# The first six steps of an attention loop in another order: value products first, the last query product behind them, two evacuations a step later

## What is computed

```
h = maximum(layernorm(x), 0)
q, k, v = h @ Wq.T + bq, h @ Wk.T + bk, h @ Wv.T + bv        # 8 heads of 32
scores  = (q @ k.T) * 32**-0.5 * (adj + adj)                  # per head, 1024 x 1024
x = x + softmax(scores) @ v @ Wo.T + bo
```

## Time and profile before

| | |
|---|---|
| median of three runs | 2977.01 us (2976.28 to 2977.42) |
| the profiled execution | 2976.45 us |
| its span, first to last instruction | 2974.6 us |
| TensorE busy | 2929.9 us (98%) |
| VectorE busy | 1869.7 us (63%) |
| ScalarE busy | 1476.8 us (50%) |
| GpSimd busy | 719.9 us (24%) |
| scores, L1292 | 1024 matmuls, 372.8 us |
| transposes, L1314 | 4096 matmuls, 539.0 us |
| masked maximum, L794 | 512, 622.5 us, 1217 ns each |
| exponential, L1050 | 512, 590.2 us, 1153 ns each |

### The profile page before, as it was taken

The page is one execution under the profiler, slowest core; times in us unless marked ns, Lnnn a source line. Parts: engine busy times, 40 slices in busy tenths (PEclk is TensorE's granted clock), DMA queues, the critical chain, the costliest instruction groups (busy, mean ns, idle before and its releaser), DMA issues.

```text
span 2974.6 us, 63498 instructions
## 1 busy us (share of the span) xinstructions
PE 2929.9 (98%) x23040; PEld 2376.7 (80%) x23040; DVE 1869.7 (63%) x4154; ACT 1476.8 (50%) x2761; POOL 719.9 (24%) x1305
## 2 busy tenths in 40 slices
PE   8999999999999999999999999999999999999999
PEld 6787787887878878788788886888868888688886
DVE  3797427974278742887428874388643886438862
ACT  1783317833178332883328732387323873238722
POOL 0343003420034201342013420134201341014410
PEclk9999999999999999999999999999999999999999
DMA  5202212022120231201311113111222021220200
GB/s 175 93 2 93 81 69 93 2 93 100 54 90 7 88 119 42 83 31 64 135 39 70 57 48 125 58 51 63 61 107 78 32 77 69 84 78 30 83 8 15
DMA packets 95317, 204.29 MB, mean 69 GB/s; under 512 B 10512, under 2 KB 41616, under 8 KB 94992
## 3 DMA queue, kind: packets, MB, share of 16 engines
q1 hardware_dynamic: 93456, 195.76, 18.0%
q0 software_dynamic: 1536, 4.20, 0.4%
HBM read 136.75 MB, written 8.65 MB: 49 GB/s over the span
## 4 chain that ended last, share of the span: by engine, by line
PE 82%; DVE 12%; ACT 3%; issue 2%; DMA 0%; DVEq 0%; ACTq 0%; SPq 0%
PE ps L1126 39%; PE ps L1314 15%; PE ps L1343 8%; PE ps L1292 8%; PE ps L1407 7%; PE ps L1482 4%; DVE junk L836 3%; DVE stats L633 1%; DVE h L852 1%; DVE dn L845 1%; DVE h L870 1%; PE ps L1166 1%; DVE shiftB L867 1%; ACT Uh L1093 1%; DVE Ul L678 1%
## 5 line engine op out<-in xcount | busy, mean ns | idle before, releaser
L794 DVE CUSTOM_DVE_ANT_0 Z<-ps,adjN 128x1024 f32<-128x1024 f32 x512 | 622.5, 1217 | 44.5 <-PE ps L1292 36.9
L1050 ACT ACTIVATE Z<-Z,nm 128x1024 f32<-128x1024 f32 x512 | 590.2, 1153 | 5.2 <-POOL nm L570 5.2
L1314 PE MATMUL ps<-ident,Z 128*128 128x128 f32 x4096 | 539.0, 275 | 2.2 <-ACT Z L1050 1.2
L1314 PEld LDWEIGHTS ps<-ident,Z 128*128 128x128 f32 x4096 | 463.7, 140 | 91.2 <-issue 42.5
L1292 PE MATMUL ps<-kS,qS 128*128 128x512 f32 x1024 | 372.8, 446 | 2.3 <-issue 1.8
L582 POOL TENSOR_SCALAR H<-adjN 128x128 fp32r<-128x128 f32 (+1 forms) x456 | 317.5, 696 | 0.0
L570 POOL TENSOR_TENSOR nm<-nm,minus 128x1 f32<-128x1 f32 x512 | 97.1, 190 | 557.0 <-DVE nm L794 556.6
L1126 PE MATMUL ps<-mh,adjT 128*128 128x256 f32 x1024 | 223.6, 379 | 0.8 <-issue 0.8
L1126 PE MATMUL ps<-v,P 128*128 128x257 f32 x1024 | 223.6, 379 | 0.0
L1126 PE MATMUL ps<-hT,t3T 128*128 128x512 f32 x512 | 221.0, 592 | 0.0
L1126 PEld LDWEIGHTS ps<-v,P 128*128 128x128 f32 x1024 | 193.9, 189 | 31.8 <-issue 3.8
(11 more groups left out here) (183 smaller groups left out, 5894.9 us busy)
## 6 DMA issues: line engine op xcount, KB each, us to landing
adjT<-adjT_in SPq DMA_DIRECT2D x8, 4096.0 KB, 13.2
adjN<-adj_in SPq DMA_DIRECT2D x8, 4096.0 KB, 17.2
adjT<-adjT_in SPq DMA_DIRECT2D x8, 2048.0 KB, 11.8
qS<-qhi SPq DMA_DIRECT2D x112, 128.0 KB, 2.1
qS<-qlo SPq DMA_DIRECT2D x112, 128.0 KB, 2.1
adjT<-adjT_in SPq DMA_DIRECT2D x8, 1536.0 KB, 6.4
xn<-x_in SPq DMA_DIRECT2D x8, 1024.0 KB, 5.8
out<-x SPq DMA_DIRECT2D x8, 1024.0 KB, 4.9
```

Of the source, the lines that this page charges most:

```text
L794: dve.tensor_tensor_reduce(Z[:, u % ZS], ps[:, 2 * (u % 2):2 * (u % 2) + 2].rearrange("p a n -> p (a n)"), adjN[:, u // HEADS], SCORE_SCAL ...
L1050: act.activation(Z[:, u % ZS], Z[:, u % ZS], ACT.Exp, bias=nm[:, u:u + 1], accum_out=sm[:, u:u + 1]).then_inc(exps.sem, 1)
L1314: mm = pe.transpose(ps[:, turn_bank((u, s)), rows(a)], Z[:, u % ZS, rows(NT // 2 * s + a)], ident[:])
```

## The change

Tables for each engine take the place of `BESIDE`. On TensorE, value products 1, 2 and 3 stand in steps 0, 2 and 3, and the last query product in step 4, where it waits for all four copies of values (it uses their bank). On ScalarE the copies of value products 1, 2 and 3 stand in steps 1, 2 and 3, each ahead of the step's evacuation. The upper part of the last query product is taken in step 5, ahead of the evacuations, and on VectorE the lower part in step 6, ahead of the evacuation of unit 3. ScalarE's evacuations of units 2 and 3 (`LATE`) are made one step later: step 3 has none, step 4 has unit 2, step 5 has units 3 and 4. The wait of value product 2 for the lower part is gone; the first weighted values wait for it instead of for the copies.

```diff
--- before.py
+++ after.py
@@ -315,10 +315,17 @@
         PARTS = (NT,)
 
 
-        BESIDE = {1: ("v", 1), 2: ("q", KQ_FIRST + 1), 4: ("v", 2), 5: ("v", 3)}
+        VALUES_AT = {0: 1, 2: 2, 3: 3}
+        COPY_VALUES_AT = {1: 1, 2: 2, 3: 3}
+        QUERY_AT, UPPER_AT, LOWER_AT = 4, 5, 6
+        LATE = (2, 3)
 
         BACK = (range(0, PTA), range(PTA, PTA + ZS), range(PTA + ZS, NT))
         STEPS = UNITS + HEADS + 3
+
+        def copied_by_act(u):
+
+            return [n for n in (u - 2, u - 1) if 0 <= n < UNITS and n + (2 if n in LATE else 1) == u]
 
         def turned(u):
 
@@ -796,8 +803,8 @@
                                                  nm[:, u:u + 1]).then_inc(zs.sem, 1)
                     if u == 1:
                         lower_kq(KQ_FIRST)
-                    if u - 2 in BESIDE and BESIDE[u - 2][0] == "q":
-                        lower_kq(BESIDE[u - 2][1])
+                    if u == LOWER_AT:
+                        lower_kq(KQ_FIRST + 1)
                     if (t := tile_due(u, NORMALISE)) is not None:
                         normalise(t)
                     if (t := tile_due(u, ADD)) is not None:
@@ -1049,15 +1056,15 @@
                         act.wait_ge(*nms(b, u + 1))
                         act.activation(Z[:, u % ZS], Z[:, u % ZS], ACT.Exp, bias=nm[:, u:u + 1],
                                        accum_out=sm[:, u:u + 1]).then_inc(exps.sem, 1)
-                    if u - 1 in BESIDE and BESIDE[u - 1][0] == "q":
-                        upper_kq(BESIDE[u - 1][1])
-                    if 1 <= u < UNITS + 1:
-                        evacuate(u - 1)
+                    if u == UPPER_AT:
+                        upper_kq(KQ_FIRST + 1)
+                    if u in COPY_VALUES_AT:
+                        copy_v(COPY_VALUES_AT[u])
+                    for n in copied_by_act(u):
+                        evacuate(n)
                     if u == 0:
                         upper_kq(KQ_FIRST)
                         copy_v(0)
-                    if u in BESIDE and BESIDE[u][0] == "v":
-                        copy_v(BESIDE[u][1])
 
                 act.activation(hh[:, :, D:HW], ones[:, 0:2 * NT].rearrange("p (t c) -> p t c", c=2), ACT.Copy).then_inc(ones_h.sem, 1)
                 for t in range(NT):
@@ -1220,8 +1227,6 @@
                         pe.wait_ge(*lasts(b, 4))
                     else:
                         pe.wait_ge(*vs(b, n))
-                    if n == 2:
-                        pe.wait_ge(*lo_s(b, len(KQ)))
                     for i in range(2):
                         mm = product(ps[:, 7, i * D:(i + 1) * D], [(hT1[:, c, rows(2 * n + i)], Wv1[:, c]) for c in range(DT)])
                     mm.then_inc(v_ps.sem, 1)
@@ -1330,7 +1335,7 @@
                         pe.wait_ge(*PT_act(b, by_act(HPG * g + HPG - 1)))
                         t = g // GROUPS
                         if g == 0:
-                            pe.wait_ge(*vs(b, NT // 2))
+                            pe.wait_ge(*lo_s(b, len(KQ)))
                         if g % GROUPS and t < NT - 1:
                             pe.wait_ge(*Rss(b, t + 1))
                         if g % GROUPS == 0 and t:
@@ -1385,13 +1390,11 @@
                     for part in range(len(PARTS)):
                         if (g := group_due(u, WEIGH + part)) is not None:
                             weighted_values(g, part)
-                    if u in BESIDE:
-                        what, n = BESIDE[u]
-                        if what == "v":
-                            project_v(n)
-                        else:
-                            pe.wait_ge(*vs(b, 2))
-                            project_kq(n)
+                    if u in VALUES_AT:
+                        project_v(VALUES_AT[u])
+                    if u == QUERY_AT:
+                        pe.wait_ge(*vs(b, NT // 2))
+                        project_kq(KQ_FIRST + 1)
                     if u > 0 and (n := turned(u)) is not None:
                         transposes(n)
                     if (t := tile_due(u, SPREAD)) is not None:
```

## The result

The changed kernel takes **2957.41 us** (median of four runs, 2953.71 to 2958.21) beside 2976.66 us of the kernel before. The ratio is 0.9936 with a 95% interval of 0.9924 to 0.9948: 19 us faster. Forecast were 2956.0 us and 2951 to 2964. The profiled execution took 2953.71 us, the lowest of the four.

The account below looks back on a forecast made before the run. TensorE, 82% of the chain, idles in each sample's first stretch. Winning 2.24 us there and 0.38 in the first tile, 2.62 per sample, 21.0 over eight, gives a median of 2956.0 us, range 2951 to 2964.

Parts of the forecast that it names:

- The first stretch: From the scores pair of unit 2 to first weighted values, per sample: 16.87 us instead of 19.11, 2.24 us won.
- the walk: Start-to-start schedule of the first sample on TensorE, ScalarE and VectorE, from measured distances: weighted values 0 at 110.74, not 112.98.
- S10: TensorE's scores pair of unit 10: at 110.10, waiting for VectorE's masked maximum of unit 8, 0.25 us behind TensorE's own list.
- The new waits: Last query product's wait for all copies: nothing, 0.47 us margin; weighted values' wait for lower half: met 3.9 us early.
- The late evacuations: ScalarE's evacuations of units 2 and 3, a step later: free, hidden by transposes and scores; otherwise 0.2 to 0.5 us each.
- the bound of 2950 us: Fastest case: waits and VectorE's chain cost nothing, TensorE's own list takes 16.14 us, 0.73 less per sample, 6 in all.
- The second term: First tile behind the first weighted values: VectorE's debt from inverting sums after exponential 7 shrinks, 0.38 us per sample won.
- rival B: Chain right, but the first tile's debt stays or value product to scores costs more: 1.9 to 2.2 us, 2961; chance 0.21.
- C: VectorE's turn 6 becomes the bound, upper half later than 105.11: if 1.25 us late, gain 11 us, 2966; chance 0.10.
- D: TensorE's clock falls in the stretch of transposes and scores behind the last query product: slower, 2986; chance 0.04.
- E: Plain loop is really held by VectorE and takes the lead back, leaving 0.5 us or less, 2973; chance 0.05.

## Why the prediction was right

**The first stretch.** Forecast 16.87 us, measured 17.11; the mis-sized term is one step of the walk. A scores pair to a product I took as 0.44 us, from two pairs and a product that took 0.99 together. Measured are 0.54 (91.39 to 91.93) and 0.55 (97.13 to 97.68), so value products 1, 2 and 3 came 0.10, 0.17 and 0.22 us later than in the walk (3.19 for 3.02 us behind S2 at the second, 6.29 for 6.07 at the third). It would have been more, but a product to the next transposes took 1.75 us (94.58 to 96.33) where I took 1.82. The copy of values 3 so stood at 8.22 us behind S2 instead of the walk's 8.00. The row I read held a product behind two pairs; the distance of one pair to what follows stood beside it in the prediction, as 0.55 to the next scores or transposes. From that copy on the walk held to the hundredth: 8.23 us from the copy of values 3 to S10 forecast (101.87 to 110.10) and measured (99.61 to 107.84), through exponential 4, evacuation 2, exponential 5, the upper half, the lower half, Z7 and Z8.

**The new waits.** The wait for all four copies ahead of the last query product cost nothing, as taken: no idle time is marked there. The weighted values' wait for the lower half cost nothing either (lower half at 103.56, weighted values at 108.50). The late evacuations were free, and the kernel without them shows that the one of unit 3 is more than free: I had priced them as a cost hidden by other work, not as what keeps the upper half early. That step was weak though not wrong: the prediction prices what they could cost, 0.2 to 0.5 us each, and not what they save. Without them 1.88 of the 2.03 us are lost.

**S10.** The prediction says that S10 comes 0.25 us later than TensorE's own list would allow. Its own steps say more: T5 at 107.49 and 0.79, 0.55 and 0.79 give 109.62, and S10 stands at 110.10, which is 0.48. Measured are 0.57 us, over three places: 0.17 at S9, 0.14 at T6 and 0.26 at S10 (0.96, 0.69 and 1.05 where plain are 0.79, 0.55 and 0.79), and taking the lower half out of the way gave back 0.54. The 0.26 at S10 alone is near the stated 0.25 by chance. The sum of TensorE's own list was wrong in the same place: the steps give 16.34 us and not 16.14, and 17.11 less 0.57 gives 16.54 as measured, so the bound of 2950 us lay too low. The forecast does not hang on either, as it went by the chain to S10.

**The second term.** Forecast 0.38 us, measured 0.38 by the sums (3.01 us over 8) and 0.40 in S13 to S14. Exponential 7 came 1.48 us ahead of the weighted values, forecast 1.36. Half of rival B, that the debt stays, fell here; its other half, a dearer step, is what happened in a small way, at S to product instead of V to S. The two together give 2.41 us per sample for 2.62, 19.3 for 21.0 us.

**The other rivals.** C had the right mechanism and not the size: the chain behind the upper half has no slack, and the kernel without late evacuations shows the price, 1.88 us lost for 1.88 us of lateness. D, the clock, did not occur: 1.00 in the 5.38 us of transposes and scores from 102.46 to 107.84. The rule in the Trainium skill, "TensorE: Matmul & The Clock Gate", section "Part 4: PE-mode transpose", that the full clock does not engage for transposes, is not borne out for this mixture. But a scores pair stands behind every eight transposes, in this stretch and in the row of 114.86 that the prediction held against the rule. What transposes alone would do no run shows. E, that the plain loop takes the lead back, fell: nothing of the lead was lost between weighted values 1 and the next sample (339.1 us on the mean for 339.3). The transfers of the second half of the queries caused no mark either.

## What to carry to other kernels

Taking a stop out of the list of the engine that ends the stretch pays only as far as no other engine's list puts it back: here the new order of products alone won 0.16 us of the first stretch, and with one evacuation made late 2.0 us. Write that engine's list down with one measured start-to-start distance per pair of operations, and then the lists of the engines that feed it, since the next bound is a sum on one of those. Look at what stands behind an instruction that must wait: moving one evacuation of 0.6 us behind the exponential and the upper half that were queued behind its wait was worth 1.9 us per sample. An edit of a loop's rhythm must be priced in its last round too, where the work beside it is of another size; keep it to the round that gains.

## What was not expected

**S2 is late in some samples**, by 0.1 to 1.2 us, and by nothing in others (0.79 us behind T0 is the plain distance). Which ones changes from run to run: three to six of eight, 2.1 to 4.6 us in all. The profile marks a transfer of key operands (kS) at some of them and "issue" at others, but the landing times say the same of all. The chain of waits of the changed kernel's first sample has

```profile
86.52 4.62 DMA kS<-klo
```

S2 starts at 91.39, 0.25 us after this landing. In the second sample SyncE issues the same transfer at 452.37, it lands at 457.30, and S2 starts at 457.39, marked "issue". In all profiles together S2 is late 57 times out of 104, and each time it starts 0.09 us (in first samples 0.24 or 0.25) after this transfer has landed; in the other 47 the transfer has landed 0.14 to 1.1 us before. These are the times from issue to landing of the transfers of kS at S2 of the second sample, which is late, and of the fourth, which is not:

```profile
DMA to landing us min/median/max: 2.1/2.9/4.9
...
DMA to landing us min/median/max: 2.1/2.5/2.9
```

The transfer takes 3.3 to 5.0 us from issue to landing where S2 is late and 2.1 to 3.3 us where it is not; why, no run shows. It was so in the kernel before too, and the change neither causes nor cures it.

**The first loop begins at 89.66 to 92.86 us**, and this goes with TensorE's granted clock ahead of it. Windows from 12 to 40 us (as above; PEclk is the third number from the end) of the kernel before, of the changed kernel's last run and of its first:

```profile
12.00:40.00 28.00, 24.32 (x114) 20.34 (x112) 6.55 (x28) 8.25 (x17) 0.27 (x1) 0.88 0.98 356
...
12.00:40.00 28.00, 25.10 (x119) 21.16 (x118) 6.99 (x30) 8.07 (x17) 0.21 (x1) 0.94 0.92 355
...
12.00:40.00 28.00, 24.59 (x127) 21.05 (x126) 6.99 (x30) 8.09 (x17) 0.21 (x1) 1.00 1.01 353
```

Their loops begin at 92.61, 91.39 and 89.66 us. In eight of the 13 profiles the mean is 0.88 and the loop begins at 92.3 to 92.9 us, in four it is 0.94 and the loop begins at 91.4 to 91.8, and in one it is 1.00. The 2.95 us between the profile before and the first one after lie between the two ends of this. Why the clock ahead of the loop differs no run shows.

Both together are of the size of the scatter of 2 to 4 us between executions of one kernel.
